# GNN residual block and two attention layers on one core: POOL's gathers and count scatters in another order, the counts one edge group later

## The reference

```python
xa  = ssp(x)
g   = einsum('pr,fr->pf', f_ij, W_att)
x_j = ssp(xa @ W_j.T + b_j)
msg = x_j[idx_j] * g
m   = x_i + segment_sum(msg, idx_i)
...
alpha = einsum('ehc,ehc->eh', q[dst], k[src]) / sqrt(C)
ex    = exp(alpha - amax[dst])
a     = ex / (denom[dst] + 1e-16)
out   = segment_sum(a * v[src], dst).mean(heads) + x @ ws + bs
```

## Time and profile before

| what | value |
|---|---|
| median of 3 runs | 3559.18 us (3556.36 to 3571.11) |
| the profiled execution | 3564.24 us, span 3562.4 us |
| mean granted TensorE clock | 0.958 |
| PE / DVE / POOL / ACT busy | 89% / 81% / 75% / 28% |
| chain that ended last | POOL 47% of the span, PE 19%, issue 17%, DVE 6%, DMA 5% |

### The profile page before, as it was taken

How to read it: one execution, slowest core, us unless ns; L and a number is a source line. 1 busy time by engine, 2 the same in 40 slices (tenths; PEclk the granted TensorE clock), 3 DMA queues, 4 the chain that set the end, 5 groups by cost and what they waited for, 6 DMA issues and landing times.

```text
span 3562.4 us, 64347 instructions
## 1 busy us (share of the span) xinstructions
PE 3187.2 (89%) x20040; PEld 1823.5 (51%) x20040; DVE 2896.8 (81%) x8886; ACT 999.1 (28%) x1689; POOL 2663.7 (75%) x1764
## 2 busy tenths in 40 slices
PE   4899999999999999999999999976788888899996
PEld 3566666666666666666666666642222222322222
DVE  6688888888888888888888888868677775877886
ACT  3111111111111111111111111133455554233433
POOL 2288888888888888888888888861787888476874
PEclk7999999999999999999999999987899999999998
DMA  8633333333333333333333333315545452232320
GB/s 311 247 49 50 45 44 50 50 50 49 50 44 45 49 50 50 49 50 46 44 49 50 50 49 50 39 2 151 151 127 150 129 151 75 78 89 76 89 64 9
DMA packets 265753, 271.38 MB, mean 76 GB/s; under 512 B 145252, under 2 KB 224717, under 8 KB 265673
## 3 DMA queue, kind: packets, MB, share of 16 engines
q1 hardware_dynamic: 90905, 163.09, 15.3%
q0 software_dynamic: 131712, 19.76, 12.7%
q10 hardware_dynamic: 43056, 87.49, 8.0%
HBM read 189.11 MB, written 81.07 MB: 76 GB/s over the span
## 4 chain that ended last, share of the span: by engine, by line
POOL 47%; PE 19%; issue 17%; DVE 6%; DMA 5%; ACT 3%; SPq 3%; POOLq 1%; DVEq 0%
POOL edge_counts L486 27%; POOL nodes_and_gaps L477 14%; PE PS L1404 6%; PE PS L1427 6%; DMA edge_counts<-small 4%; POOL scores L541 4%; PE PS L1436 3%; SPq L366 2%; POOL counts_and_logs L524 1%; DVE scores L1142 1%; DVE PS L1153 1%; DVE counts_and_logs L1128 1%; PE PS L1416 1%; DMA edge_counts<-counts_and_logs 1%; ACT scores L729 1%
## 5 line engine op out<-in xcount | busy, mean ns | idle before, releaser
L1303 PE MATMUL PS<-scores 128*128 128x320 bf16 x11760 | 1707.2, 303 | 132.5 <-DVE scores L974 69.1
L1303 PEld LDWEIGHTS PS<-scores 128*128 128x128 bf16 x11760 | 1156.9, 99 | 664.4 <-DVE scores L974 160.5
L486 POOL DMA_INDIRECT edge_counts<-small x752 | 1211.6, 1611 | 282.0 <-issue 282.0
L541 POOL TENSOR_TENSOR scores<-scores,max_of_targets 125x896 f32<-125x896 f32 x335 | 701.5, 2140 | 191.4 <-ACT max_of_targets L724 142.0
L477 POOL DMA_INDIRECT nodes_and_gaps<-xj_rows,small x588 | 580.9, 988 | 242.4 <-issue 162.8
L974 DVE TENSOR_SCALAR scores<-scores,small 128x192 bf16<-128x192 bf16 x3136 | 748.2, 304 | 3.5
L889 DVE SCALAR_TENSOR_TENSOR scores<-scores,small,PS 128x512 bf16<-128x512 f32 x784 | 573.0, 731 | 0.0
L1142 DVE TENSOR_TENSOR scores<-PS,counts_and_logs 125x896 f32<-125x896 f32 x350 | 377.8, 1082 | 204.0 <-PE PS L1404 76.9
L624 ACT ACTIVATE scores<-nodes_and_gaps 128x512 bf16<-128x512 f32 x98 | 61.7, 630 | 1403.6 <-DVE nodes_and_gaps L952 929.8
L729 ACT ACTIVATE scores<-scores 125x896 f32<-125x896 f32 x350 | 329.9, 948 | 372.8 <-POOL scores L541 365.9
L1404 PE MATMUL PS<-q_features,k_features 64*125 64x448 f32 x1400 | 371.1, 612 | 68.0 <-DVE scores L1142 65.1
(11 more groups left out here) (192 smaller groups left out, 2124.0 us busy)
## 6 DMA issues: line engine op xcount, KB each, us to landing
counts_and_logs<-edge_counts SPq DMA_DIRECT2D x70, 980.0 KB
scores<-tile_keys ACTq DMA_DIRECT2D x96, 512.0 KB
edge_counts<-counts_and_logs SPq DMA_DIRECT2D x50, 766.0 KB
edge_counts<-counts_and_logs SPq DMA_DIRECT2D x35, 980.0 KB
running_max<-fetch_targets ACTq DMA_DIRECT2D x48, 312.5 KB
max_of_targets<-fetch_targets ACTq DMA_DIRECT2D x48, 312.5 KB
edge_counts<-small POOLq DMA_INDIRECT x752
nodes_and_gaps<-xj_rows,small POOLq DMA_INDIRECT x588
```

The costliest lines, as they stand in the source:

```text
L486: pool.indirect_dma_start(cnt_dram, bass.IndirectOffsetOnAxis(ap=index[:, s:s + 1], axis=0), value[:, s:s + 1], None, compute_op=ALU.add). ...
L541: nc.gpsimd.tensor_tensor(t, t, MB, ALU.subtract).then_inc(sem("shifted"), 1)
L1303: ins = nc.tensor.matmul(PS[:, b, 0:HI * F], onehot[:, s, b * P:b * P + 128], spread[:, s, i].rearrange("p h f -> p (h f)"), start=first a ...
```

## The change

`BEHIND` becomes 5, so the counts of group g - 5 are scattered in group g. The order in a group becomes 3 gathers, 4 scatters, 3 gathers, 4 scatters. The wait for the staged counts stands behind the first three gathers, and the wait for the clearing stands in front of the first scatter of all (group 0, tile 0), which is in group 5. The groups 0 to 4 have gathers alone, group 5 is written out, and the loops of POOL and DVE begin with group 6 (`FRONT`). The last 5 groups of scatters follow the loop. The column pairs are chosen by `(u + BEHIND) % 2`, so that a group of counts keeps its parity.

```diff
-BEHIND = 4
+BEHIND = 5
+FRONT = BEHIND + BEHIND % 2
...
             def scatter(h, s, index, value):
 
+                if isinstance(h, int) and h == s == 0:
+                    pool.wait_ge(sem("counts_cleared"), 16 * FILLS)
                 if s % ROUND == 0:
                     pool.wait_ge(sem("count_added"), 16 * G * h + 16 * s)
                     settled()
...
             def group(g, u, scatters):
                 pool.wait_ge(sem("targets_staged"), g + 1)
-                if scatters:
-                    pool.wait_ge(sem("counts_staged"), 2 * (g - BEHIND) + 2)
                 settled()
+                b = (u + BEHIND) % 2
                 for s in range(0, G, ROUND):
-                    if scatters:
-                        for e in range(ROUND):
-                            scatter(g - BEHIND, s + e, cidx[u], cnt[u])
                     for e in range(ROUND):
                         if s + e not in FETCHED:
                             gather(g, u, s + e)
+                    if scatters and s == 0:
+                        pool.wait_ge(sem("counts_staged"), 2 * (g - BEHIND) + 2)
+                        settled()
+                    if scatters:
+                        for e in range(ROUND):
+                            scatter(g - BEHIND, s + e, cidx[b], cnt[b])
 
             pool.wait_ge(sem("xj_stored"), 32)
             for g in range(BEHIND):
                 group(g, g % 2, False)
-            pool.wait_ge(sem("counts_cleared"), 16 * FILLS)
-            with pool.Fori(BEHIND // 2, NG // 2) as k:
+            for g in range(BEHIND, FRONT):
+                group(g, g % 2, True)
+            with pool.Fori(FRONT // 2, NG // 2) as k:
                 for u in range(2):
                     group(2 * k + u, u, True)
...
                 if counts is not None:
-                    stage_counts(g + 2 - BEHIND, u, counts)
+                    stage_counts(g + 2 - BEHIND, (u + BEHIND) % 2, counts)
...
-            for g in range(BEHIND):
+            for g in range(FRONT):
                 edge_group(g, g % 2, g // 2, g == 0, None if g < BEHIND - 2 else g == BEHIND - 2)
-            with dve.Fori(BEHIND // 2, NG // 2 - 1) as k:
+            with dve.Fori(FRONT // 2, NG // 2 - 1) as k:
```

## The result

The changed kernel takes 3643.76 us (median of 4 runs, 3638.79 to 3650.37), beside 3560.27 us of the kernel before on the same chip: a ratio of **1.0231** (95% interval 1.0202 to 1.0259), 83 us **slower**. The prediction was 3535 us and faster. It missed its range by 96 us, on the side to which it gave 0.08.

The account below looks back on a forecast made before the run. POOL was taken to pace the loop at 23.05 us a group, DVE close behind. An attention stage 25.2 us earlier, with 0.7 us taken off, gave -24.5 us on the 3559.18 us median: 3535 us, range 3519 to 3548.

Parts of the forecast that it names:

- The head: Before the loop: nine gathers fit POOL's idle stretch, last gathers end 34.6 us earlier, DVE's 20.66 us wait goes.
- DVE's own pace: DVE in the loop: taken as 22.5 us a group, so it closes its lag behind POOL in ten groups.
- The new wait: DVE's staging of counts: waits for landed scatters, keeping DVE about 9 us behind POOL; takes back 6.7 of 34.6 us.
- The loop body: POOL in the loop: same instructions and waits, landings covered by three gathers, still 23.05 us a group, cost 0.
- Rival B: Loop: the new wait makes DVE and PE the bound at 23.61 us a group, 27.7 us later, 3587 us; chance 0.08.
- Rival C: POOL in the loop: mean scatter time shifts by 0.04 us, giving 3519 us or about no gain; chance 0.12.
- The tail: Behind the loop: ten scatter rounds take 94.1 us, ending 7.8 us earlier; the attention stage starts 25.2 us earlier.

## Why the prediction was wrong

**The head.** Right: nine gathers by 140.35 us, first scatter at 154.86, messages of group 4 at 156.35 us without a wait.

**DVE's own pace.** 22.5 us was taken. From group 4 to group 5 it took 21.19 us, and (243.00 - 156.35) / 4 = 21.66 us a group up to group 8. So DVE closed the gap by group 8 and not after ten groups. The size was off and the consequence right: from group 8 on, at 243.00 us, the wait at the staging stands there.

**The new wait.** Its place, its releaser and its presence in nearly every group were right. The step asked what the wait does to DVE, and rightly found nothing (1.75 us of it cost nothing where the loads were moved). It did not ask what else hangs on DVE's phase. ACT's loads do, and so do POOL's instructions that run beside DVE's.

**The loop body.** This step failed, and it decided the sign: "The same instructions, the same number of waits for landed scatters, each still covered by three gathers. POOL's 23.05 us stay. [...] Cost 0." A landing that takes 1.7 us is covered by three gathers; one that shares the DMA engines with 0.9 MB takes 4.8 us and is not. It cost 0.96 us a group in waits, and 0.30 us more in longer gathers. Over the 88 groups from 8 to 96 that is 88 x 1.2 = 106 us, against 24.5 us of forecast gain. The trace of before held the loads in ACT's queue and their 6 us of traffic; the prediction never placed them against the rounds, as it had not looked at the DMA engines as a resource. The Trainium skill says, in DMA: Bandwidth & Descriptors (Issuing engines are not separate DMA queues), that transfers started by different engines run on the same 16 DMA engines and interleave. The landing of 4.8 us beside 1.7 us, and POOL's wait that is gone with 0.3 MB less, agree with it.

**Rival B** had the right sign and a time that was too low (3587 us), and the wrong mechanism: POOL never waited for staged targets or counts, and DVE's stall cost nothing by itself. **Rival C** ("POOL's own pace moves") came nearest, 0.04 us on every scatter bringing "the sum back to about zero". It was measured as 0.05 us on every gather, and the prediction had not thought of the waits. The third gather of a half and the scatter behind it stood in the place where DVE begins its pieces, 1.25 and 1.82 us in the timeline above, beside 0.94 and 1.62 us in the timeline of the kernel before with the loads six matches later. Why they are longer there stays open. The Trainium skill, SBUF — State Buffer (SBUF: two separate sides), says that GpSimd cannot write the descriptors of its DMAs while DVE runs an instruction in a mode that takes the port the two share. The durations would agree; that it is this port, and that DVE's instructions there run in such a mode, was not shown by a run.

**The tail.** Ten rounds were taken as 94.1 us; from 2404.05 to 2497.8 us they took 93.7. Where the body's pace was restored by the staging in another place, the time was 3534.78 us for 3535 predicted. That this is so close is in part luck, as that version is not the predicted one and its terms differ: the last messages start at 2286.75 us and not at 2297.4, the counts' loads go out at 2394.25 us and not at 2400.7, DVE waits 7.6 us for the logarithm and not 4, and the first steepening is 30.3 us earlier than before and not 25.2, while the profiled execution is 27.3 us shorter.

**The rest of the difference.** 78.5 us at the first steepening, 74 us in the span. Behind it nothing was looked for.

## What to carry to other kernels

When an edit changes which engine waits for which, place every transfer that is timed by the engine that gets pinned against every wait for a landing, not only the instructions: a transfer's landing time is no constant but depends on what shares the DMA engines in those microseconds. A wait that costs its own engine nothing may still lock two streams into the one phase in which they collide, in every iteration, where a free-running kernel meets it in none. Try moving the wait a few instructions down its queue before giving up the change: here that turned 83 us lost into 19 to 25 us won. And run the parts of a change alone: the old order with five groups behind won 22.5 us with no other edit.

## What was not expected of the hardware

- A round of four scatters, each of 128 words, had landed 1.7 us after the end of its last descriptor row alone and 4.8 us after it with 0.9 MB of loads beside it. The cost had a narrow window: 0.8 to 2.0 us for loads issued 1 to 3 us ahead of the round's end, 0.2 to 0.4 us at 3 to 4, 0.2 us within the last microsecond, none over 4 us ahead or 1 to 3 us behind.
- GpSimd's issue of one gather took 0.94 to 1.25 us by what stood beside it; pinned to the bad place in each group this was some 31 us of the kernel, by the mean gather of 1.041 for 0.986 us.
- The same version ran with DVE waiting for the gathers, 1.7 us behind them, in one profiled execution and trailing them by 14 us over the whole loop in another. Its gain was 25 us in the one measurement and 19 in the other; how much of the 6 us the lag made, and what decides between the two, stays open.
